# Second attention of a four-block model: four weighings placed in front of the next quad's fourth transposed score

## What is computed

```python
c_kv = hidden_states @ w_dkv.T
q = (hidden_states @ w_q.T).reshape(B, S, HEADS, HEAD_DIM)     # 16 heads of 16
k = (c_kv @ w_uk.T).reshape(B, S, HEADS, HEAD_DIM)
v = (c_kv @ w_uv.T).reshape(B, S, HEADS, HEAD_DIM)
scores = jnp.einsum('bqhd,bkhd->bhqk', q, k) * scale
scores = scores + alibi_bias(S)[None, None]                    # causal, a slope by distance
attn = jax.nn.softmax(scores, axis=-1)
out = jnp.einsum('bhqk,bkhd->bqhd', attn, v).reshape(B, S, HIDDEN)
return out @ w_o.T
```

## Time and profile before

| | |
|---|---|
| median of 3 runs | 2847.7 us (2835.64 to 2851.89) |
| profiled execution | 2841.48 us, span 2839.6 us |
| mean granted TensorE clock | 0.908 of full |
| busy over the span | PE 2335.7 (82%), DVE 1783.8 (63%), ACT 1678.7 (59%), POOL 704.2 (25%) |
| second attention's scores and weighings | about 2096 to 2576 us |
| the part with scores and weighings at the full clock | 2157 to 2508 us |

### The profile page before, as it was taken

One profiled execution on the slowest core, in us unless ns is written; L12 is line 12 of the kernel. 1 busy time (PEld: TensorE's weight loads), 2 busy tenths in 40 slices (PEclk: granted clock), 3 DMA queues, 4 the chain that ended last, 5 costly groups with the idle time before them and its releaser, 6 DMA issues. The chain is left out here.

```text
span 2839.6 us, 42530 instructions
## 1 busy us (share of the span) xinstructions
PE 2335.7 (82%) x12560; PEld 1566.7 (55%) x12561; DVE 1783.8 (63%) x3726; ACT 1678.7 (59%) x3051; POOL 704.2 (25%) x974
## 2 busy tenths in 40 slices
PE   4954585556999999999999997986639999997985
PEld 2532253225877787877777885554315444434653
DVE  4786669673777677767776776523347778823523
ACT  2776667673877777777777765232306777763232
POOL 0213420342422332133225322154010000000153
PEclk9977897787999999999999998998858999977998
DMA  1011101014100000000001001223360303000124
GB/s 47 0 38 45 53 22 37 37 52 136 31 16 12 21 21 15 12 24 16 16 8 31 8 1 59 77 78 115 132 99 1 46 2 46 2 1 3 53 80 135
DMA packets 78250, 115.62 MB, mean 41 GB/s; under 512 B 24658, under 2 KB 52146, under 8 KB 75058
## 3 DMA queue, kind: packets, MB, share of 16 engines
q1 hardware_dynamic: 67796, 91.62, 11.6%
q0 software_dynamic: 10240, 21.38, 2.5%
HBM read 70.63 MB, written 41.94 MB: 40 GB/s over the span
## 5 line engine op out<-in xcount | busy, mean ns | idle before, releaser
L1389 DVE TENSOR_TENSOR aa_pt_lo<-psum,aa_pt_hi 128x512 fp32r<-128x512 f32 x544 | 350.5, 686 | 82.6 <-ACT aa_pt_hi L1319 80.0
L1840 DVE TENSOR_REDUCE ab_part_max<-psum 128x2 f32<-128x1024 f32 (+3 forms) x320 | 327.3, 1062 | 116.4 <-PE psum L1678 114.4
L1782 ACT ACTIVATE ab_prob<-psum 128x512 f32<-128x512 f32 (+3 forms) x640 | 298.0, 542 | 121.2 <-PE psum L1707 117.1
L1319 ACT ACTIVATE aa_pt_hi<-psum 128x512 fp32r<-128x512 f32 x544 | 297.4, 598 | 116.2 <-PE psum L1249 113.3
L1376 DVE CUSTOM_DVE_ANT_0 aa_prob<-psum,bias 128x512 f32<-128x512 f32 (+2 forms) x480 | 278.7, 598 | 113.2 <-PE psum L1239 93.9
L1237 PE MATMUL psum<-ka_hi,aa_q_hi 128*128 128x512 f32 (+3 forms) x640 | 267.9, 419 | 11.1 <-POOL aa_q_lo L1171 8.3
L1203 POOL TENSOR_TENSOR x<-aa_y_out,x 128x256 f32<-128x256 f32 x256 | 188.2, 735 | 353.4 <-ACT aa_y_out L1337 308.7
L1249 PE MATMUL psum<-ident,aa_prob 128*128 128x128 f32 x1600 | 253.0, 274 | 6.8 <-issue 5.5
L1707 PE MATMUL psum<-ab_q_stack,ab_k_stack 50*128 50x512 f32 (+3 forms) x640 | 243.7, 460 | 13.2 <-ACT ab_prob L1782 8.8
L1311 ACT ACTIVATE aa_prob<-aa_prob,aa_neg_max 128x128 f32<-128x128 f32 (+11 forms) x192 | 228.0, 1188 | 43.8 <-DVE aa_neg_max L1382 42.0
L1260 PE MATMUL psum<-aa_pt_hi,c_stack 128*128 128x512 f32 x544 | 233.6, 429 | 5.9 <-ACT aa_out_t L1326 4.3
(11 more groups left out here) (334 smaller groups left out, 4922.8 us busy)
## 6 DMA issues: line engine op xcount, KB each, us to landing
q_rows<-ixt_q_out SPq DMA_DIRECT2D x64, 256.0 KB, 2.1
aa_q_row<-q_rows SPq DMA_DIRECT2D x64, 256.0 KB, 2.6
f_back<-done SPq DMA_DIRECT2D x16, 512.0 KB, 7.6
w<-in_w SPq DMA_DIRECT2D x6, 896.0 KB, 11.3
x<-in_hidden SPq DMA_DIRECT2D x2, 2048.0 KB, 11.5
ab_q_stack<-stash_q_hi SPq DMA_DIRECT2D x32, 128.0 KB, 10.4
ab_k_stack<-stash_k_hi SPq DMA_DIRECT2D x32, 128.0 KB, 11.9
ixt_wq_n<-in_Wq_nope_T SPq DMA_DIRECT2D x2, 1024.0 KB, 5.6
```

The costliest lines, as they stand in the source:

```text
L1319: nc.scalar.activation(pt_hi[(TB[t] + j) % RING][:], turn_bank[(TB[t] + j) % RING], ACT.Copy).then_inc(pt_hi_done, 1)
L1389: nc.vector.tensor_tensor(pt_lo[ring][:], turn_bank[(TB[t] + j) % RING], pt_hi[ring][:].bitcast(F32), ALU.subtract).then_inc(pt_lo_done, 1)
L1782: nc.scalar.activation(prob[i % 2][h][:, 0:w], t_bank[slot % RING][:, 0:w], ACT.Exp).then_inc(t_taken, 1)
L1840: nc.vector.tensor_reduce(part_max[e % 2][:, at:at + 5:4, part], s_pair[pair % 2][:, :, 0:w], AX.X, ALU.max).then_inc(s_used, 1)
```

## The change

The four "weigh" steps of quad i - 1 are put into the list ahead of the transposed score t3 of quad i, where they stood behind t3 and the score s2. The list of each iteration is then t0, s1, t1, s0, t2, s3, the four weighings, t3, s2, and at chunk ends keep, turn and flip as before. It holds for the iterations 1 to 160; in the last, which has no transposed scores, the weighings stand alone in either version. Nothing else is altered.

```diff
         for i in range(ALL + 3):
             fresh = scores(i + LEAD)
             for h in range(GB):
+                if h == GB - 1 and 1 <= i <= ALL:
+                    steps += [("weigh", i - 1, n) for n in range(GB)]
                 if i < ALL:
                     steps.append(("t", i, h))
                 steps += fresh[h:h + 1]
             if 1 <= i <= ALL:
-                steps += [("weigh", i - 1, h) for h in range(GB)]
                 if (i - 1) % NQ in ENDS:
                     steps.append(("keep", (i - 1) // NQ * NCH + ENDS.index((i - 1) % NQ)))
             steps += turns(i + LEAD - 1)
```

## The result

The changed kernel took 2925.8 us (median of 4 runs, 2908.06 to 2928.79) against 2848.6 for the kernel before, now also of 4 runs: a ratio of **1.0267, 95% interval 1.0237 to 1.0296**. The profiled execution took 2926.15 us with a span of 2923.9.

A forecast was written before the change was run, and what follows sets the result against it. A ring of TensorE and ScalarE was taken to bound wide quads at 2.60 us, with VectorE close behind. The profiled 2841.5 us + 52 + 0 = 2893.5, plus 6.2 to the median, gave 2900, range 2868 to 2945.

The forecast's parts named there:

- The bank ring: Transposed scores waiting for exponentials to empty their 3 banks: stays 2.60 us per wide quad wherever the train stands; counted nothing.
- The pair of scores: Main stretch: s3 waits for the maximum of s3 and s2, now with the train between: 3.22 us per wide quad against 2.60.
- The sum for the 135 quads: Main stretch: maxima, hand-overs, trains, masks and transposes together take 403 us against 351, so +52.
- the clock: Rival, chance 0.13: lower clock in the main stretch; 2931 for a hundred microseconds of it, 3094 for the whole stretch.
- the forecast's own case: Whole kernel slower through the split pair of scores, chance 0.74: 2900 us, from 2868 to 2928 without the mild clock case.
- 1.44 of 4.66: Wide quad of the main stretch at the lower clock: 4.66 us, of which 1.44 is added by that clock.
- The weight load: Weighing's load in front of the train: kept in the ring; taken out, 0.18 less per quad and +28, not +52.
- TensorE's waits for exponentials: Main stretch, a sign: fall from 110.9 us to under 60 and stand before t2, not t3.
- its first rival: Main stretch and end: t3's wait for its exponential is simply hidden, so faster, 2820 us; chance 0.06.
- The waits for the maxima: Main stretch, a sign: s3 and its mask wait 50 to 80 us for the maximum in place of some 9.
- The end (4.04): Last 19 quads, without fresh scores: wide quads keep 4.04 us, change 0; the last quad under +1.
- the 6 first quads: Quads ahead of the main stretch, at the lower clock: +1 us, bounds 0 and 4.

The follow-up runs named there:

- e2: Changed kernel with the four weighings one place further to the front, before t2, between s0 and s3: 2856.3 us, ratio 1.001.
- e3: Changed kernel with score s3 moved behind the weighings and t3, next to s2: 2847.4 us, ratio 1.001 to the kernel before.
- e5: Changed kernel with the weighings two places further to the front, before t1, between s1 and s0: 2969.8 us, ratio 1.043.
- e6: Changed kernel with each row maximum taken over only the first half of its block's columns: 2841.4 us, ratio 0.998 to the kernel before.
- e0: Not a run: the first exponential of a quad, on ScalarE; its start marks where the quad begins in the timings.
- e8: Changed kernel with scores s1 and s0 computed twice where no mask is added: 2907.0 us, ratio 1.022 to the kernel before.
- e1: The changed kernel run again, unaltered: 2928.8 us, ratio 1.026 to the kernel before.
- e4: Changed kernel with t3 put back ahead of the weighings, leaving s2 alone behind them: 3006.0 us, ratio 1.055 to the kernel before.
- e10: e9 with the lead-in's scores also computed twice where no mask is added: 2832.9 us, ratio 0.995 to the kernel before.
- e9: Kernel before with one unused score added beside each transposed score of the last 19 quads: 2829.5 us, ratio 0.995.

## Why the prediction was right, and where it wasn't

**The bank ring, counted at nothing: right.** Its length hardly depends on where the train stands: e2 and e3 have the train at two new places and give 2.64 and 2.59, and the last quads keep 4.04.

**The pair of scores: right in mechanism and in size.** 3.22 was worked out for a wide quad, and 3.26 measured where no mask stands in it: s2 to its maximum is 0.56 and not 0.54, the maximum's end to s3 0.06 and not 0.05. At the full clock the 135 quads would take 405 us, where 403 was forecast. e3 takes the loss away by mending the pair alone, e5 brings it with the other pair, e6 shortens the ring by what the maximum gives up. One reading under the sum was too simple: 2.60 is the length of the wide quads and, by chance, also about the mean of the stretch. From e0 to e0 the quads 256 and 128 wide took 2.15 and 2.27 us on average in the kernel before, and the 512-wide ones 2.68 with the turns and chunk ends among them, so 2.60 doesn't hold in every quad as the bank ring's floor.

**The sum for the 135 quads: short by 22 us** (+52 against +74.4). The term that was mis-sized is the clock, put at nothing in the sum and given 0.13 as a separate case, with prices for a hundred microseconds or the whole stretch; only the upper end of the range allowed for a mild form. It came as a small part of the forecast's own case: five drops, 54.5 us in all, worth 19 us (17 by the prediction's 1.44 of 4.66 per microsecond). Of the prediction's own signs of being wrong, "if the clock drops" so came true in part.

That the clock is a consequence of the idle time is supported by e3, e6 and e8, though not proved: it stays at 1.00 where the ring is short, and is less often low where work fills the wait. The traces also show where it falls. Seven kernels have falls in the 135 quads (after, e1, e2, e4, e5, e8, e10), 31 in all, and every one begins in a quad of transposed scores narrower than 512 or at most two quads behind one, as in the changed kernel at 2432.6 us, in the first quad behind three narrow ones (columns of the first table of stretches):

```profile
2421.00:2432.00 11.00, 9.95 (x98) 5.27 (x98) 7.23 (x9) 5.58 (x17) 0.00 (x0) 1.00 0.01 1
2433.00:2442.00 9.00, 8.97 (x45) 4.06 (x49) 4.24 (x5) 5.10 (x12) 0.00 (x0) 0.50 0.00 0
```

The thin stretch in the earlier trace rows that had kept 1.00, the prediction's argument against a drop, lies in just such narrow quads: it was one stretch of 4 us, and too little to go by.

**The weight load that the prediction would take out of the ring by the Trainium skill's rule (TensorE: Matmul & The Clock Gate, "Step-by-step: what each phase is for"): it stayed in.** From s3's load to the train's is 0.42 to 0.43 in the rows of the changed kernel too, with s3 alone (its weights load at 2361.51, the train's at 2361.93):

```profile
2361.51 0.18 PEld L1679 LDWEIGHTS psum<-ab_k_stack,ab_q_stack 49*128 49x128 f32 x1 [0.23 <-DVE ab_part_max L1841]
...
2361.93 0.13 PEld L1720 LDWEIGHTS psum<-ab_prob,values 128*17 128x17 f32 x8 [0.24 <-issue]
```

So the lower end of that term (0.18) was needless width. It doesn't speak against the rule either: a weighing's weights take all 128 rows, so they share rows with the score in flight, and the rule's first condition, row groups that don't conflict, isn't met. Whether its second, the background buffer, could be, no run shows. The prediction's +28 by that rule had not asked this.

**TensorE's waits for exponentials: wrong.** I expected them to fall from 110.9 to under 60; they are 129.5 in the longer stretch (waits of the changed kernel from 2160 to 2590 us):

```profile
PEld psum L1708 <- ACT ab_prob L1783: 100.2, 145, 1.7
PEld psum L1706 <- ACT ab_prob L1783: 29.3, 66, 1.3
```

The row counts idle time of the weight loader, and the 0.85 ahead of each t0 in the earlier trace rows is the train itself, during which no weights but the weighings' are loaded. Of the 129.5 us, 84.6 stand directly behind a train, and of the 110.9 before 74.8. So two thirds of what is put down to ScalarE is TensorE's own streaming, and the prediction was wrong to read the 110.9 us as waiting, above all in the case for its first rival. The waits for the maxima came close: 45.1 in the weight loader's two rows (the rows of PE count partly the same idle time again), where 50 to 80 were expected. The end (4.04) and the 6 first quads (20.1 us against 23.2: the clock rose some 8 us behind the first e0, in the kernel before 23) moved the total by no more than the bounds given.

## What to carry to other kernels

A move in a hand-written order is to be followed round every ring that passes the moved block, not only the one whose wait it is meant to fill: a ring of banks with one train in it kept its length here wherever the train stood (2.59 to 2.64), while a second ring gained the whole train as soon as it landed between the two halves of something that is released together. Keep what one instruction consumes (here a pair of scores) contiguous in the producer's order. Count a loss of density on TensorE twice: once as waiting, and once as stretches at the lower clock, which here made about a quarter of the loss.

## What the runs showed of the hardware that I had not expected

The clock fell inside a stretch in which TensorE had work every 3.3 us (0.94 mean, five times), each time in or within two quads behind the narrow ones of a chunk end, and the more the longer the quads were: 0, 10, 54, 126 and 188 us at the lower level for mean quads of 2.59, 2.68, 3.14, 3.44 and 3.73 us, though length and clock feed each other. Each microsecond at the lower level cost 0.35 us in the changed kernel and in e4, the quads at the full clock being the measure. Added matmuls with no use made the kernel faster by 20 us in its last quads (e9). The same means did nothing in the lead-in (e10), where only scores run, between waits for maxima; why it is not enough there stays open.
